# Projection and binarised FFN of a conv-attention model: two group-wise phases replaced by one software pipeline with a column-tiled second layer

## What is computed

```python
t = t + _L1_attn_ref(_ln_t(t), ...)      # ends in: out @ Wp + bp
t = t + _L1_ffn_ref(_ln_t(t), W1, b1, W2, b2)
...
def _quantize_activations_groupwise(x):  # NUM_GROUPS = 5, QB = 128, EPS = 1e-5
    gs = x.shape[0] // NUM_GROUPS
    xq = jnp.zeros_like(x)
    for g in range(NUM_GROUPS):
        ag = x[g * gs:(g + 1) * gs]
        gamma = jnp.max(jnp.abs(ag))
        xq = xq.at[g * gs:(g + 1) * gs].set(jnp.clip(ag * QB / (gamma + EPS), -QB + EPS, QB - EPS))
...
h = _bitlinear(x, W1, b1)                # 96 -> 384, signs of W, quantised as above
h = jax.nn.gelu(h, approximate=False)
out = _bitlinear(h, W2, b2)              # 384 -> 96
```

## Time and profile before

| | us |
|---|---|
| median of 3 runs | 3175.21 |
| the profiled execution | 3178.23 |
| its span | 3176.5 |
| `project_and_ffn` within it | from 2546.2 to the end |

### The profile page before, as it was taken

The page is one execution under the profiler, slowest core; times in us unless marked ns, Lnnn a source line. Parts: engine busy times, 40 slices in busy tenths (PEclk is TensorE's granted clock), DMA queues, the critical chain, the costliest instruction groups (busy, mean ns, idle before and its releaser), DMA issues. The chain is left out here.

```text
span 3176.5 us, 82271 instructions
## 1 busy us (share of the span) xinstructions
PE 2933.0 (92%) x27166; PEld 1732.6 (55%) x27166; DVE 2279.5 (72%) x4553; ACT 2072.6 (65%) x3922; POOL 1003.0 (32%) x1911
## 2 busy tenths in 40 slices
PE   4899999999999499999999999999999988988986
PEld 2445455454544266666666666666666643453442
DVE  3566666656666389898889888898889745665665
ACT  1667777777776367777777777777777745645644
POOL 0143444434344444444434444444444300000000
PEclk8999999999999789999999999999999988988998
DMA  1112222322331377666666666666666431131231
GB/s 31 40 50 97 78 104 70 103 96 77 104 103 60 122 127 119 114 114 118 119 114 114 117 118 117 112 117 118 117 115 114 77 81 37 53 89 35 54 89 40
DMA packets 892557, 291.92 MB, mean 92 GB/s; under 512 B 844081, under 2 KB 877138, under 8 KB 892498
## 3 DMA queue, kind: packets, MB, share of 16 engines
q1 hardware_dynamic: 889042, 290.37, 41.5%
q10 hardware_dynamic: 3456, 0.79, 0.1%
HBM read 101.55 MB, written 88.08 MB: 60 GB/s over the span
## 5 line engine op out<-in xcount | busy, mean ns | idle before, releaser
L941 DVE TENSOR_REDUCE at_unit_max<-at_ps_queries 128x1 f32<-128x512 f32 (+3 forms) x2304 | 1121.1, 548 | 120.2 <-PE at_ps_queries L833 97.8
L907 ACT ACTIVATE at_probs<-at_ps_keys 128x512 f32<-128x512 f32 x1344 | 738.4, 596 | 245.2 <-PE at_ps_keys L847 217.1
L833 PE MATMUL at_ps_queries<-at_turned 96*128 96x512 bf16 (+3 forms) x2304 | 688.4, 330 | 35.0 <-DMA at_turned<-at_spread 32.4
L847 PE MATMUL at_ps_keys<-at_turned 128*128 128x128 bf16 (+3 forms) x3456 | 668.9, 275 | 2.2 <-ACT at_probs L907 2.0
L847 PEld LDWEIGHTS at_ps_keys<-at_turned 128*128 128x128 bf16 x3456 | 255.4, 97 | 240.7 <-ACT at_probs L907 122.4
L867 PE MATMUL at_ps_values<-at_probs,at_v 128*32 128x128 f32 x10752 | 373.4, 276 | 0.5 <-ACT at_probs L907 0.5
L836 PE MATMUL at_ps_queries<-mask_queries,ident_bf 128*128 128x128 bf16 x1536 | 339.2, 221 | 0.0
L867 PEld LDWEIGHTS at_ps_values<-at_probs,at_v 128*32 128x32 f32 x10752 | 270.9, 110 | 42.3 <-ACT at_probs L907 1.3
L833 PEld LDWEIGHTS at_ps_queries<-at_turned 96*128 96x128 bf16 x2304 | 217.6, 98 | 101.4 <-DMA at_turned<-at_spread 33.4
L801 POOL TENSOR_TENSOR at_tick<-at_one 128x1 f32<-128x1 f32 x192 | 37.0, 193 | 693.2 <-ACT at_diag_probs L907 453.1
L907 ACT ACTIVATE at_diag_probs<-at_ps_keys 128x512 f32<-128x512 f32 x384 | 208.5, 595 | 12.2 <-PE at_ps_keys L847 4.1
(11 more groups left out here) (202 smaller groups left out, 4807.6 us busy)
## 6 DMA issues: line engine op xcount, KB each, us to landing
qkv_rows<-cb_packed SPq DMA_DIRECT2D x32, 1536.0 KB, 8.2
at_stacks<-qkv_rows SPq DMA_DIRECT2D x192, 256.0 KB, 3.3
cb_x<-in_x_dram SPq DMA_DIRECT2D x32, 384.0 KB, 3.7
cb_x_again<-in_x_dram SPq DMA_DIRECT2D x32, 384.0 KB, 4.6
x_after_conv<-cb_x SPq DMA_DIRECT2D x32, 384.0 KB, 5.1
attention_rows<-at_att SPq DMA_DIRECT2D x384, 32.0 KB, 2.1
ff_att_rows<-attention_rows SPq DMA_DIRECT2D x32, 384.0 KB, 3.9
ff_x<-x_after_conv SPq DMA_DIRECT2D x32, 384.0 KB, 4.6
```

Of the source, the lines that this page charges most:

```text
L833: mm = pe.matmul(pq[:, u % QBANKS, 0:n], QT[0:STACK, slot, qb * P:(qb + 1) * P], KT[0:STACK, slot, k0:k0 + n], start=True, stop=True)
L847: mm = pe.matmul(pk[:, bank_k, c0:c0 + n * P], KT[:, slot, kb * P:(kb + 1) * P], QT[:, slot, q0 * P:(q0 + n) * P], start=(c0 == 0), stop=True,
L907: act.activation(probs, pk[:, (slot * NU + k) % KBANKS, :], ACT.Exp, scale=scale).then_inc(S["probs"], 1)
L941: dve.tensor_reduce(MX[:, r % 2, qb, k0 // BANK:k0 // BANK + 1], pq[:, u % QBANKS, 0:n], AX.X, ALU.max).then_inc(S["unit_max"], 1)
```

## The change

The two phases and the loop over groups go. All engines walk over rounds r from -2 on, straight-line code with no loop. In round r batch n = r+2 is projected, m = r+1 is normalised, r goes through the first layer, s = r-6 through the second layer (so a group's last first-layer batch is out before its second layer begins), and o = r-13 is put out. The second layer works in four column tiles: each product has 32 output channels (one of three blocks b), 256 tokens (one of four quarters q) and writes to the 32 partitions of its quarter, all into the PSUM tile `out`. Y2 and the output so lie as 128 partitions by 3x256. To meet that layout X2 is stored to DRAM (`x_after_attention`) and loaded again in quarters. The second-layer bias is loaded in this stage in four small DMAs, no longer in `prepare`. The root and the reciprocal become one power of -0.5 on GpSimd (the epsilon is a 97th column of the squares), and both caps go to GpSimd. X2 has 3 slots instead of 6, Y1 and Y2 have 7; the maxima of both scales use a corner of `centred`.

What the tiles and semaphores become, and SP's order (the diff's lines inside the function are shown with twelve blanks less, removed lines are in the listing above, the loops of before are replaced as a whole):

```diff
-def project_and_ffn(nc, w, att, x1, y_out):
+def project_and_ffn(nc, w, att, x1, x2, y_out, b2):
...
+FULL = GROUPS * GB
+LAG = GB
+OUT_LAG = 2 * GB + 1
+QP, QT = C // 3, L // 4
+SLOTS = GB + 1
...
+X2 = sb("x2", [C, 3, L])
+SQ = sb("squares", [P, TILES, C + 1])
...
+XN = sb("xn", [P, TILES, C])
...
+Y1 = sb("hidden", [P, SLOTS, CHUNKS, L])
+Y2 = sb("ffn", [P, SLOTS, 3, QT])
+XR = sb("x2_again", [P, 4, 3, QT])
+OUT = sb("out", [P, 4, 3, QT])
...
+M1, M2 = sb("group_max1", [P, GROUPS, 4]), sb("group_max2", [P, GROUPS, 4])
+B2 = sb("b2", [P, 3])
...
+row_ps, spread_ps = pc[0:1, BANK - P:BANK], pc[:, 2 * BANK - 1:2 * BANK]
 a_loaded = [sem(f"att_loaded{i}") for i in range(2)]
 x_loaded = [sem(f"x1_loaded{i}") for i in range(2)]
...
+x2_stored = [sem(f"x2_stored{i}") for i in range(3)]
+xr_loaded = [sem(f"x2_again_loaded{i}") for i in range(4)]
+stored = [sem(f"stored{i}") for i in range(4)]
+b2_loaded = sem("b2_loaded")
...
+def quarters(dram):
+return dram.rearrange("(b c) (q t) -> q c b t", c=QP, t=QT)
...
+    def load(n):
+        sp.dma_start(AR[:, n % 2, :, :], att[n].rearrange("(t p) c -> p t c", p=P)
+                     ).then_inc(a_loaded[n % 2], 16)
+        sp.dma_start(X1[:, n % 2, :], x1[n]).then_inc(x_loaded[n % 2], 16)
+    load(0)
+    load(1)
...
+        for q in range(4):
+            sp.dma_start(B2[q * QP:(q + 1) * QP, :], b2.rearrange("(b c) -> c b", c=QP)
+                         ).then_inc(b2_loaded, 16)
+    for r in range(-2, FULL + OUT_LAG):
+        n, s = r + 2, r - OUT_LAG
+        if n < BATCH:
+            sp.wait_ge(S["att_turned"], n + 1)
+            sp.wait_ge(S["x2_ready"], n + 1)
+            if n + 2 < BATCH:
+                load(n + 2)
+            sp.dma_start(x2[n] if n < FULL else y_out[n], X2[:, n % 3, :]).then_inc(x2_stored[n % 3], 16)
+        m = s + 2
+        if 0 <= m < FULL:
+            _above(sp.wait_ge, S["out_ready"], m - 3)
+            sp.wait_ge(x2_stored[m % 3], 16 * (m // 3 + 1))
+            for q in range(4):
+                sp.dma_start(XR[q * QP:(q + 1) * QP, m % 4, :, :], quarters(x2[m])[q]
+                             ).then_inc(xr_loaded[m % 4], 16)
+        if s >= 0:
+            sp.wait_ge(S["out_ready"], s + 1)
+            for q in range(4):
+                sp.dma_start(quarters(y_out[s])[q], OUT[q * QP:(q + 1) * QP, s % 4, :, :]
+                             ).then_inc(stored[s % 4], 16)
```

TensorE's order:

```diff
     pe.wait_ge(S["ones_set"], 2)
...
+    def hidden(n, k):
+        for a in range(2):
+            _above(pe.wait_ge, S["y1_copied"], 6 * n + 2 * k + a - 1)
+            pe.matmul(pf[:, a * BANK:(a + 1) * BANK], w["w1"][:, k * P:(k + 1) * P],
+                      XNT[:, a * BANK:(a + 1) * BANK], start=True, stop=True).then_inc(S["y1_psum"], 1)
+    def row_of_maxima(M, g, name, all_name):
+        pe.wait_ge(S[name], 2 * g + 1)
+        pe.transpose(row_ps, M[:, g, 0:1], w["ident"][:, :]).then_inc(S[all_name], 1)
+    def spread_max(M, g, name, all_name):
+        pe.wait_ge(S[name], 2 * g + 2)
+        pe.matmul(spread_ps, ROW[:, :], M[0:1, g, 1:2], start=True, stop=True).then_inc(S[all_name], 1)
+    for r in range(-2, FULL + LAG + 1):
+        n, m, s = r + 2, r + 1, r - LAG
+        if 0 <= r < FULL:
+            pe.wait_ge(S["xn_ready"], r + 1)
+            pe.wait_ge(S["att_copied"], r + 2)
+            for t in range(TILES):
+                mm = pe.transpose(pt[0:C, t * P:(t + 1) * P], XN[:, t, :], w["ident"][:, :])
+            mm.then_inc(S["xn_turned"], 1)
+        if r >= GB and r % GB == 0 and r <= FULL:
+            spread_max(M1, r // GB - 1, "max1", "all_max1")
+        if 0 <= m < FULL:
+            pe.wait_ge(S["x2_ready"], m + 1)
+            for t in range(TILES):
+                if t == 4 and r >= GB and r % GB == 0:
+                    pe.wait_ge(S["scale1"], 2 * (r // GB) - 1)
+                if t == 4 and r >= OUT_LAG and r % GB == 1:
+                    pe.wait_ge(S["scale2"], 2 * (r // GB) - 3)
+                c0 = (t // 4) * BANK + (t % 4) * C
+                mm = pe.matmul(pc[:, c0:c0 + C], X2[:, m % 3, t * P:(t + 1) * P], w["centre"][:, :],
+                               start=True, stop=True)
+            mm.then_inc(S["xc_done"], 1)
+        if 0 <= r < FULL:
+            pe.wait_ge(S["xnt_ready"], r + 1)
+            hidden(r, 0)
+        if n < BATCH:
+            pe.wait_ge(a_loaded[n % 2], 16 * (n // 2 + 1))
+            _above(pe.wait_ge, S["att_copied"], n)
+            for t in range(TILES):
+                mm = pe.transpose(pt[0:C, t * P:(t + 1) * P], AR[:, n % 2, t, :], w["ident"][:, :])
+            mm.then_inc(S["att_turned"], 1)
+        if 0 <= r < FULL:
+            hidden(r, 1)
+        if n < BATCH:
+            pe.wait_ge(S["att_copied"], n + 1)
+            _above(pe.wait_ge, S["x2_ready"], n)
+            _above(pe.wait_ge, S["y2_ready"], s)
             for a in range(2):
...
+                half = slice(a * BANK, (a + 1) * BANK)
+                mm = pe.matmul(py[0:C, half], w["wp"][:, :], AT[:, half], start=True, stop=True)
+            mm.then_inc(S["y_done"], 1)
+        if 0 <= r < FULL:
+            hidden(r, 2)
+        if r >= 2 * GB and r % GB == 0:
+            if m < FULL:
+                pe.wait_ge(S["xn_ready"], m + 1)
+            row_of_maxima(M2, r // GB - 2, "max2", "all_max2")
+        if 0 <= s < FULL:
+            pe.wait_ge(S["x2_ready"], min(n + 1, BATCH))
+            _above(pe.wait_ge, S["y2_ready"], s)
             for k in range(CHUNKS):
...
+                pe.wait_ge(S["h_ready"], 3 * s + k + 1)
+                for b in range(3):
+                    for q in range(4):
+                        mm = pe.matmul(py[q * QP:(q + 1) * QP, b * QT:(b + 1) * QT],
+                                       w["w2"][:, k, b * QP:(b + 1) * QP],
+                                       Y1[:, s % SLOTS, k, q * QT:(q + 1) * QT], start=(k == 0 and b != 1),
+                                       stop=(k == CHUNKS - 1), skip_group_check=True)
             mm.then_inc(S["y2_psum"], 1)
...
+        if r % GB == GB - 1 and 0 <= r < FULL:
+            if m < FULL:
+                pe.wait_ge(S["xn_ready"], m + 1)
+            row_of_maxima(M1, r // GB, "max1", "all_max1")
+        if r >= 2 * GB and r % GB == 0:
+            spread_max(M2, r // GB - 2, "max2", "all_max2")
```

ScalarE's order:

```diff
+    act.wait_ge(b2_loaded, 64)
+    def copies(n, k):
+        for a in range(2):
+            act.wait_ge(S["y1_psum"], 6 * n + 2 * k + a + 1)
+            act.activation(Y1[:, n % SLOTS, k, a * BANK:(a + 1) * BANK], pf[:, a * BANK:(a + 1) * BANK],
+                           ACT.Copy).then_inc(S["y1_copied"], 1)
+    def gelu(s, k):
+        g = s // GB
+        act.wait_ge(S["scale1"], 2 * g + 2)
+        act.activation(Y1[:, s % SLOTS, k, :], Y1[:, s % SLOTS, k, :], ACT.Gelu,
+                       scale=M1[:, g, 3:4]).then_inc(S["gelu"], 1)
+    for r in range(-2, FULL + LAG + 1):
+        n, m, s = r + 2, r + 1, r - LAG
+        if 0 <= r < FULL:
+            act.wait_ge(S["xn_turned"], r + 1)
+            act.activation(XNT[0:C, :], pt[0:C, :], ACT.Copy).then_inc(S["xnt_ready"], 1)
+        if 0 <= s - 1 < FULL:
+            act.wait_ge(S["y2_psum"], s)
+            _above(act.wait_ge, S["out_ready"], s - SLOTS)
+            for b in range(3):
+                ins = act.activation(Y2[:, (s - 1) % SLOTS, b, :], py[:, b * QT:(b + 1) * QT],
+                                     ACT.Identity, bias=B2[:, b:b + 1])
+            ins.then_inc(S["y2_ready"], 1)
+        if 0 <= m < FULL:
+            act.wait_ge(S["xc_done"], m + 1)
+            act.activation(SQ[:, :, 0:C].rearrange("p (a t) c -> p a t c", a=2),
+                           xc.rearrange("p a (t c) -> p a t c", c=C), ACT.Square, scale=C ** -0.5).then_inc(S["squares"], 1)
+        if 0 <= r < FULL:
+            copies(r, 0)
+        if n < BATCH:
+            act.wait_ge(S["att_turned"], n + 1)
+            _above(act.wait_ge, S["y_done"], n)
+            act.activation(AT[:, :], pt[0:C, :], ACT.Copy).then_inc(S["att_copied"], 1)
+        if 0 <= r < FULL:
+            copies(r, 1)
+        if 0 <= s < FULL and s % GB == 0:
+            gelu(s, 0)
+            gelu(s, 1)
+        if 0 <= r < FULL:
+            copies(r, 2)
+        if 0 <= s < FULL and s % GB == 0:
+            gelu(s, 2)
+        if 0 <= s + 1 < FULL and (s + 1) % GB:
+            for k in range(CHUNKS):
+                gelu(s + 1, k)
```

GpSimd's order (new; in front of it, two small memsets set MINUS_HALF to -0.5 and column C of SQ to 1e-5):

```diff
+    def limit(s, k):
+        pool.wait_ge(S["gelu"], 3 * s + k + 1)
+        pool.tensor_scalar(Y1[:, s % SLOTS, k, :], Y1[:, s % SLOTS, k, :], LIMIT, None, ALU.min
+                           ).then_inc(S["h_ready"], 1)
...
+    for r in range(-1, FULL + OUT_LAG):
+        m, s, o = r + 1, r - LAG, r - OUT_LAG
+        if 0 <= m < FULL:
+            pool.wait_ge(S["var_sums"], m + 1)
+            _above(pool.wait_ge, S["xn_ready"], m)
+            pool.tensor_tensor(SCALE[:, :], VS[:, :], MINUS_HALF[:, :], ALU.pow).then_inc(S["scale"], 1)
+        if o >= 0:
```

(77 more changed lines are left out.)

228 lines of the change are left out of this document (16 added, 212 removed).

## The result

The changed kernel takes 3134.22 us, the median of 4 runs (3126.59 to 3136.65), against 3174.35 us (3170.60 to 3177.16) for the kernel before: ratio 0.987, 95% interval 0.9849 to 0.9891. The forecast was 3047 us in a range of 3035 to 3100. The sign was right; the gain is 40 us where 128 were forecast.

The account below looks back on a forecast made before the run. TensorE was taken to bound rounds and second layers, with a four-engine chain at turnovers. Opening, rounds, group starts, tail and end summed to 502.0 us against 630.3, giving 3047 us; 8-in-10 range 3035 to 3100.

Parts of the forecast that it names:

- the prices on GpSimd: Per operation on GpSimd: hidden cap 1.1 us, output cap 1.0, power 0.5.
- Full rounds: Rounds 6 to 29, both layers: 14.5 us each, 348.0 in all; the chain to X2 just fits beside TensorE.
- p: Time of GpSimd's power in the chain into X2: taken as 0.5 us, bounds 0.2 to 1.5.
- rival (b): GpSimd's power bounds the round, costing p-0.7 in 30 rounds; p of 1 to 5 us chance 0.14, above 0.05.
- Group starts: Four tiny products and a Gelu delayed by the scale: 1.75 us per group, 7.0 for four; 3.4 each with slower caps.
- Rounds 31 to 35: Tail with second layer only: 4.0 us plus an unhidden eviction of 1.3, so 5x5.3 = 26.5 us.
- The end: After the last scale: SP alternates stores and loads at 1.4 us each, 21.0 us in all.
- Opening and rounds 0 to 5: Opening 22.9 us, including 1.0 for the bias wait (bounds 0 and 3); six first-layer-only rounds of 10.39, 62.4.
- The column tiles: Second layer on TensorE: 72 records, four side by side, 4.0 us per batch; bounds 3.8 and 15.5.
- rival (a): Second-layer tiles not fully side by side: about 5.0 us at 3.07x, chance 0.10; one by one 3392 us, chance 0.01.
- The turnovers: Gaps between groups, 24.3 us before, vanish from the middle because the scale is worked out under the next round.
- Rival (d): TensorE's clock falls in rounds 31 to 35, 4 us more each, 3067 us; chance 0.11 shared with small waits.

Follow-up runs that it names:

- experiment 3: Changed kernel with hidden and output caps on VectorE and a hidden maximum between sum of squares and xn; GpSimd keeps only the power: 3058.11 us.
- experiments 2 and 5: Each against the changed kernel. 2: first hidden maximum moved between VectorE's sum and xn, 3116.67 us. 5: GpSimd's power and hidden cap made products, 3117.12 us.
- Experiment 1: Changed kernel with the hidden caps back on VectorE, root and output cap still on GpSimd: 3074.49 us, ratio 0.9685.
- experiment 4: Changed kernel with ScalarE's bias wait moved from its first instruction to the first eviction needing it: 3129.23 us, ratio 0.9865.
- Experiment 8: experiment 3 plus the late bias wait of experiment 4, and six X2 reload slots loaded four batches ahead instead of two: 3047.43 us.

## Why the prediction was wrong

**The step that failed is the prices on GpSimd.** For the hidden cap the prediction has "nearest 1.09 (one input, 1024 elements), upper 2.0": it took 2.77, above its own upper bound. I took the row nearest in form, and that row is attention's `TENSOR_SCALAR_AFFINE_SELECT`, another operation; the bound was scaled from a two-input product, as if one input could only be cheaper. The same cap on VectorE takes 0.69, which experiment 3 shows, so GpSimd is 4 times as slow. The Trainium skill (GPSIMD Engine Reference, 4.1 Engine selection) puts it otherwise, "1-input is roughly line-rate". These rows, 2.77 against 0.69 us, do not agree with it. The output cap took 2.99 on average (2.86 alone) where I took 1.0 without a row, and the power 1.66 where I took 0.5 between bounds of 0.2 and 1.5, again outside.

**Where the 86 us between 502.0 and 588.4 lie:**
- Full rounds: the walk has a slack up to p = 0.7, and "beyond, each us of p adds one to a round". With p = 1.66 that is 0.96; TensorE starts the second layer 0.93 late, and the round takes 15.4 for 14.5. Over 24 rounds 22 us. The mechanism and the place were right, and the slack near enough; experiments 2 and 5 bring the shortest full rounds to 14.57 by taking only the power's wait away. It was rival (b), at 0.19 in all, with a p that I held for unlikely. Its price took 30 rounds, but rounds 1 to 4, which have no second layer, are not longer for it.
- Group starts: 7.0 forecast for four. Measured are 29.8 us over plain rounds: 10.0 for the first (40.8-2x15.4), then 6.9, 5.6 and 7.3. The larger part is three caps of 2.77 in a row between the Gelu and the second layer: TensorE waits for them 5.1 us in round 6 and 3.5 in round 12. In the round after, the power stands behind the last cap, and VectorE waits 2.99 for it, not 1.80. Some 7 us are the lower clock: 3.5 in round 6, after the gap of 2.24 us, and 1.7 in each of rounds 13 and 25, where the second layer takes 5.78, not 4.09. In experiment 3 the three later starts cost 1.3 each. The prediction priced caps of up to 2.0 there, 3.4 in all, and looked at the first round of a group only.
- Rounds 31 to 35: 5.3 forecast from TensorE and an eviction, 11.04 measured from four GpSimd operations, 29 us; round 30 and the last scale are 2.7 over. The sum of GpSimd's work was held against the full round of 14.5 only, never against these. With the prices right but that step omitted, these 29 us would have been missed all the same; with 2.77 in it, it is arithmetic: 3x2.74+2.86 = 11.1. Experiment 1 gives 5.45.
- The end: 26.0 for 21.0. Six output caps stand one behind the other, 20.96 us in the window's row or 3.5 each, longer than the 2.86 of the tail, all but the first with one of VectorE's additions beside it. Experiment 3, caps on VectorE, takes 23.1, and there the forecast's own term shows: SP's four stores or loads take 1.73 to 1.88 each time, not 1.4. Experiment 8, two of the four reloads out of the way, 19.0.
- Opening and rounds 0 to 5: 6.4 us over. The bias wait was named, at 1.0 with an upper bound of 3; it took 3 (experiment 4: 25.0 to 21.7). Rounds 1 to 4 are 10.41, forecast 10.39. The first (12.07) runs partly at the lower clock, and the sixth (12.96) waits 2.24 us for the row of maxima, which the sum had left out.

**What held.** The column tiles: 4.03 us from start to start for 72 records, forecast 4.0, and not the 5.0 of rival (a). A TensorE-bound round of 14.4, measured 14.57 once GpSimd is out of its chain. The turnovers are gone. Rival (d), a falling clock in the tail, did not come: 1.00 in experiment 8 at a busy share of 0.67; the 0.78 in the changed kernel's tail stands beside TensorE idle for half of the time. But the argument against it, a full clock "in every stretch at this or higher load", misread: one of them has TensorE busy for 7.00 of 7.00 us at a clock of 0.74, and the falls at group starts above were in no rival. And the terms as a whole: experiment 8, whose GpSimd does only the power, has a stage of 504.3 against 502.0, though that is partly luck, as 4.9 us more in rounds 6 to 29 and 3.2 more in rounds 0 to 5 are made up by an opening, a tail and an end that are 2.4, 1.4 and 2.0 shorter.

**What stays open.** How long the clock stays low after round 5's gap differs between executions: 3.5 us lost in the changed kernel, 5.2 in experiment 3. Why it falls in round 13 and in round 25 of the changed kernel and not in round 19, after nearly the same waits, no run shows. Covering that row of maxima was not tried.
